# Mixture-of-experts layer behind a cross attention: first units of four experts taken from the first six batches

## The reference, cut to what matters

```python
x = x + xattn(layernorm(x), ctx, ctx, ctx)          # x: 8 x 100 x 512, ctx: 8 x 722 x 512
x = x + ffn(layernorm(x), router_w, w1, b1, w2, b2)

def xattn(x, w1, v1, w2):
    h = gelu_tanh(einsum('eth,efh->etf', x, w1)) * einsum('eth,efh->etf', x, v1)
    return einsum('etf,efh->eth', h, w2)

def ffn(h, router_w, w1, b1, w2, b2):               # 16 experts, w1: 512 x 1024, w2: 1024 x 512 each
    logits = x @ router_w                           # x: 800 tokens x 512
    assign = argmax(logits)                         # one expert for each token
    w = sigmoid(logits[assign])
    return w * (gelu(x @ w1[assign] + b1[assign]) @ w2[assign] + b2[assign])
```

## Time and profile before

| | |
|---|---|
| median of 3 runs | 310.06 us (309.59 to 310.96) |
| the profiled execution | 313.14 us, its span 311.4 us |
| TensorE | 246.1 us busy, 79% of the span |
| VectorE / GpSimd / ScalarE | 120.0 / 98.8 / 32.1 us busy |
| moved by DMA | 100.41 MB, mean 322 GB/s |
| mean granted TensorE clock | 0.917 of full speed |

### The profile page before, as it was taken

One profiled execution on the slowest core, in us unless ns is written; L12 is line 12 of the kernel. 1 busy time (PEld: TensorE's weight loads), 2 busy tenths in 40 slices (PEclk: granted clock), 3 DMA queues, 4 the chain that ended last, 5 costly groups with the idle time before them and its releaser, 6 DMA issues.

```text
span 311.4 us, 10067 instructions
## 1 busy us (share of the span) xinstructions
PE 246.1 (79%) x3668; PEld 172.9 (56%) x3669; DVE 120.0 (39%) x405; ACT 32.1 (10%) x75; POOL 98.8 (32%) x141
## 2 busy tenths in 40 slices
PE   0899999999999884397778877987984678859850
PEld 0858768768678351154456665655663456536540
DVE  3034536446444466133334333444433134324320
ACT  0411111021021120010010101010110011000100
POOL 2002314224123155003523334435343133241353
PEclk9999999999999955597999979999999599977995
DMA  7999799999999994089699968999999999999910
GB/s 258 370 372 355 271 343 360 372 309 408 336 394 380 400 376 160 26 290 385 200 352 378 372 221 302 355 367 364 378 362 388 361 422 362 390 361 388 354 36 21
DMA packets 20698, 100.41 MB, mean 322 GB/s; under 512 B 5232, under 2 KB 6224, under 8 KB 11464
## 3 DMA queue, kind: packets, MB, share of 16 engines
q1 hardware_dynamic: 15044, 93.02, 81.2%
q0 software_dynamic: 4928, 6.60, 6.7%
q10 hardware_dynamic: 708, 0.55, 0.6%
HBM read 95.58 MB, written 4.97 MB: 323 GB/s over the span
## 4 chain that ended last, share of the span: by engine, by line
PE 47%; DMA 24%; issue 10%; SPq 9%; DVE 2%; POOL 2%; POOLq 2%; ACTq 2%; DVEq 1%; ACT 0%
PE bank L308 14%; PE bank L315 14%; DMA W<-in_w 10%; DMA area<-rows 10%; PE bank L396 8%; SPq L228 8%; PE bank L385 5%; PE bank L323 2%; DMA id_out<-tok_at 2%; DMA rows<-nothing,pad_at 1%; ACTq L209 1%; PE bank L404 1%; PE bank L293 1%; PE bank L299 1%; DMA xs<-in_x 1%
## 5 line engine op out<-in xcount | busy, mean ns | idle before, releaser
L385 PE MATMUL bank<-W,area 128*32 128x256 f32 x992 | 66.5, 405 | 23.2 <-DMA W<-in_w 12.0
L396 PE MATMUL bank<-W,area 128*32 128x128 f32 x1984 | 65.8, 287 | 3.9 <-issue 3.0
L396 PEld LDWEIGHTS bank<-W,area 128*32 128x32 f32 x1984 | 56.0, 115 | 9.2 <-issue 4.2
L795 POOL DMA_INDIRECT out<-area,at_out x32 | 32.7, 1022 | 85.5 <-DVE area L672 49.4
L385 PEld LDWEIGHTS bank<-W,area 128*32 128x32 f32 x992 | 34.1, 115 | 45.4 <-issue 25.6
L315 PE MATMUL bank<-area,hidT 128*100 128x512 f32 (+1 forms) x96 | 46.8, 601 | 0.0
L308 PEld LDWEIGHTS bank<-xnT,area 128*128 128x128 f32 (+1 forms) x384 | 44.3, 193 | 4.3 <-issue 4.3
L308 PE MATMUL bank<-xnT,area 128*128 128x100 f32 (+1 forms) x384 | 44.6, 278 | 1.0 <-issue 1.0
L491 ACT ACTIVATE area<-area 128x256 f32<-128x256 f32 x31 | 12.9, 416 | 172.5 <-PE bank L396 150.7
L209 POOL DMA_DIRECT2D area<-rows x32 | 24.5, 765 | 18.3 <-issue 18.2
L672 DVE SCALAR_TENSOR_TENSOR area<-bank,area 128x128 f32 x31 | 10.9, 351 | 42.7 <-PE bank L396 24.5
(11 more groups left out here) (86 smaller groups left out, 156.4 us busy)
## 6 DMA issues: line engine op xcount, KB each, us to landing
W<-in_w SPq DMA_DIRECT2D x64, 1024.0 KB, 18.6
area<-in_ctx_main SPq DMA_DIRECT2D x8, 1280.0 KB
area<-in_ctxT_a SPq DMA_DIRECT2D x8, 768.0 KB, 10.0
area<-in_ctxT_b SPq DMA_DIRECT2D x8, 676.0 KB, 9.2
area<-rows POOLq DMA_DIRECT2D x32, 65.5 KB, 7.2
xs<-in_x SPq DMA_DIRECT2D x8, 200.0 KB
area<-in_ctx_rest SPq DMA_DIRECT2D x8, 160.0 KB
out<-area,at_out POOLq DMA_INDIRECT x32
```

The lines of the kernel that those rows point to most:

```text
L385: last = nc.tensor.matmul(p_h[U * q:U * q + U, 0:FQ], curT[:, U * k:U * k + U], mine, start=(k == 0), stop=(k == KD - 1), tile_position=(0 ...
L396: last = nc.tensor.matmul(p_y[U * q:U * q + U, 0:DQ], hT[:, U * c:U * c + U], W2[:, slot, c, DQ * q:DQ * q + DQ], start=(c == 0), stop=(c ...
L795: nc.gpsimd.indirect_dma_start(out_q, bass.IndirectOffsetOnAxis(ap=at_out[r][:, :], axis=0), y_out[:, r, :], None, bounds_check=last_out, ...
```

## The change

- **Head units.** When batches 0 to 5 are routed, the first 32 rows of experts 0 to 3 are fixed as units 0 to 3 (where an expert has fewer than 32 by then, `end_head` raises its counter so that later tokens go behind them; rows that nobody filled were zeroed at the start). GpSimd loads them in the batch loop, and their steps stand between the steps of the last batch's routing on TensorE, VectorE and ScalarE.
- **Plan.** The planned units follow as units 4 and up: experts 0 to 3 have at least one more each. The plan is computed on 44 partitions at once, and `colof` and its tables are gone.
- **Output index.** Each row carries the index of its output row, so `tok_at`, its scatters and the load of `id_out` are gone. `XW` grows from 131 to 132.
- **Row loads.** SyncE, not GpSimd, loads the rows of the planned units, expert by expert, before the weights of this expert.
- **Weights.** All 16 early halves are issued in the batch loop (`EARLY` ends in 7, not 2).
- **Tail.** Nothing is loaded behind the last unit. GpSimd handles the last one or two units through a third output buffer, one after the other.

With the counts above experts 0 to 3 now have 3, 2, 2 and 5 units (before: 3, 1, 2 and 5), the others as before, so there are 32 units.

The diff, cut to its core:

```diff
-EARLY = (0, 0, 1, 1, 1, 2, 4, 2)
+EARLY = (0, 0, 1, 1, 1, 2, 4, 7)
...
         @block.sync
...
+            def load_rows(e, slot, head):
+                at = slice(e, e + 1) if isinstance(e, int) else bass.ds(e, 1)
+                n = sp.value_load(n_i[0:1, at], min_val=1, max_val=PER)
+                start = sp.value_load(starts[0:1, at], min_val=SLOTS, max_val=MAXU - 1)
+                with sp.Fori(0, n) as u:
...
+                    sp.dma_start(xr[:, bass.ds(at, 1), :].rearrange("p o d -> p (o d)"),
+                                 rows[bass.ds(CAP * e + U * u + (U if head else 0), U), :].rearrange(
+                                     "t (q d) -> q t d", q=Q)).then_inc(s_rows[slot], 16)
+
+            def rows_landed(e, slot):
+                at = slice(e, e + 1) if isinstance(e, int) else bass.ds(e, 1)
+                sp.wait_ge(s_rows[slot], sp.value_load(slot_n[0:1, at], min_val=16, max_val=16 * MAXU))
+                sp.sem_inc(s_land, 1)
+
             sp.wait_ge(s_att, NB)
-            load_weights(2)
-            sp.wait_ge(s_land, AHEAD)
-            load_weights(4 * SLOTS - sum(EARLY) - 2)
-
-
+            sp.wait_ge(s_b2ps, len(p_b2))
             sp.wait_ge(s_plan, 1)
+            for i in range(2):
+                sp.wait_ge(s_row[i], 16 * (NB // 2))
+            for e in range(SLOTS):
+                sp.wait_ge(s_pad[e // Q], 16)
+                load_rows(e, e, True)
+                if e > 0:
+                    rows_landed(e - 1, e - 1)
+            for i in range(1, PADS):
+                sp.wait_ge(s_pad[i], 16)
+
+
             with sp.Fori(1, E // SLOTS) as g:
                 for s in range(SLOTS):
...
+                    load_rows(sp.snap(SLOTS * g + s), s, False)
                     sp.wait_ge(s_hp, before)
+                    apart()
+                    rows_landed(SLOTS * g + (s - 1), (s - 1) % SLOTS)
                     load_half(W1[:, s], first, s_w1[s], 0)
                     load_half(W1[:, s], first, s_w1[s], 1)
                     sp.wait_ge(s_y, before + 1)
+                    apart()
                     load_half(W2[:, s], second, s_w2[s], 0)
                     load_half(W2[:, s], second, s_w2[s], 1)
+            rows_landed(E - 1, SLOTS - 1)
...
         @block.tensor
...
-            transpose_x2(NB - 1)
-            logits(NB - 1)
-            ranks(NB - 1)
-            nc.tensor.matmul(p_lg[:, 0:E], ones, hot_sum[:, :], start=True, stop=False)
-            nc.tensor.matmul(p_lg[:, 0:E], ones, hot[:, :], start=False, stop=True).then_inc(s_cntps, 1)
...
+            pe.sem_inc(s_y, 1)
             transpose_tokens(0)
-            pe.wait_ge(s_tab, 7)
-            pe.sem_inc(s_y, 1)
+            pe.wait_ge(s_b2, 16)
+            spread_b2(0)
+            first_layer(0, 0, 16)
+            transpose_x2(NB - 1)
+            transpose_tokens(1)
+            spread_b2(1)
+            logits(NB - 1)
+            first_layer(1, 1, 16)
+            ranks(NB - 1)
+            nc.tensor.matmul(p_lg[:, 0:E], ones, hot_sum[:, :], start=True, stop=False)
+            nc.tensor.matmul(p_lg[:, 0:E], ones, hot[:, :], start=False, stop=True).then_inc(s_cntps, 1)
+            transpose_tokens(2)
+            spread_b2(2)
+            pe.wait_ge(s_b2v, 1)
+            spread_b2(3)
+            second_layer(0, 0, 16)
+            first_layer(2, 2, 16)
+            transpose_tokens(3)
+            second_layer(1, 1, 16)
+            first_layer(3, 3, 16)
+            pe.wait_ge(s_tab, 9)
+            pe.wait_ge(s_pos, NB)
+            nc.tensor.transpose(p_rk[0:1, 0:MAXU], done_n[:, :], ident[0:MAXU, 0:MAXU]).then_inc(s_eofps, 1)
+            second_layer(2, 2, 16)
+            transpose_tokens(4)
+            pe.wait_ge(s_plan, 1)
...
         @block.scalar
...
             copy_rows(p_t, tT, s_tps, s_tT, NB - 1)
             gate_tanh(NB - 1)
...
+            nc.scalar.activation(warm[:, :], con[0:1, 0:1], ACT.Gelu)
+            for j in range(3):
+                gelu_unit(j)
+            act.wait_ge(s_plan, 1)
+            n = units(act)
+            with act.Fori(3, n) as j:
+                gelu_unit(j)
...
         @block.vector
...
+            def end_head():
+                dve.wait_ge(s_headps, 1)
+                nc.vector.tensor_scalar(short[:, :], p_rk[0:1, 0:SLOTS], -1.0, float(U), ALU.mult, ALU.add
+                                        ).then_inc(s_short, 1)
...
+            next_tokens(0)
+            residual(NB - 1)
+            tokens(0)
+            x2_moments(NB - 1)
+            b2_copy(0)
+            next_tokens(1)
+            hidden_units(0)
+            tokens(1)
...
+            biases(0)
+            next_tokens(2)
+            b2_copy(1)
+            route(NB - 1)
+            hidden_units(1)
+            place(NB - 1)
+            pads()
+            tokens(2)
+            biases(1)
+            finish(0, 0)
+            next_tokens(3)
+            plan()
+            hidden_units(2)
+            tokens(3)
+            biases(2)
+            experts()
+            finish(1, 1)
...
+            b2_copy(2)
+            b2_copy(3)
+            next_tokens(4)
+            hidden_units(3)
+            tokens(4)
+            biases(3)
+            finish(2, 0)
...
         @block.gpsimd
...
+                if b == HEAD_END:
+
+                    pool.wait_ge(s_att, HEAD_END + 1)
+                    for i in range(2):
+                        pool.wait_ge(s_row[i], 16 * (HEAD_END // 2))
+                        apart()
+                    for e in range(SLOTS):
+                        pool.dma_start(xr[:, e, :], rows[CAP * e:CAP * e + U, :].rearrange("t (q d) -> q t d", q=Q)
+                                       ).then_inc(s_pre[e], 16)
...
-            unit(0, None, 0)
-            unit(1, None, 1)
-            pairs = pool.snap((n + 1) // 2)
+            for r in range(2):
+                scatter_unit(r, r, None)
+            pool.wait_ge(s_plan, 1)
...
+            with pool.Fori(0, left) as k:
+                scatter_unit(2 * pairs + k, 2, None)
+                pool.wait_ge(s_done[2], 16 * k + 16)
+                apart()
```

More of the change, by code:

```diff
@@ L123, in build @@
         pos = [sb(f"pos{i}", [T, 1], U32) for i in range(2)]
[L124 to L130, removed]
+        short = sb("short", [1, SLOTS])
@@ new lines, in build @@
+        need, end_f = sb("need", [MAXU, E]), sb("end_f", [MAXU, E])
+        done, done_n = sb("done", [MAXU, E]), sb("done_n", [MAXU, 1])
+        n_i, ends, starts = sb("n_i", [MAXU, E], I32), sb("ends", [1, E], I32), sb("starts", [1, E], I32)
+        slot_f, slot_n = sb("slot_f", [1, E]), sb("slot_n", [1, E], I32)
+        eof, last_but_two = sb("eof", [1, MAXU], I32), sb("last_but_two", [1, 1], I32)
+        last_unit, out_at = sb("last_unit", [1, 1], I32), [sb(f"out_at{i}", [P, 1], U32) for i in range(3)]
@@ L151, in build, with part @@
[L151 to L154, removed]
+        used = 0
+        def part(n):
+            nonlocal used
+            used += n
+            return area[:, used - n:used]
+        cur, curT = part(DQ), part(KD * U)
+        h_pre, hT = part(KF * U), part(KF * U)
+        y_out = part(3 * DQ).rearrange("p (r d) -> p r d", r=3)
@@ L579, in _ @@
                     place(b - 1)
-                residual(b)
+                if b + 1 < NB:
+                    residual(b)
+                    x2_moments(b)
                 if b == 0:
@@ L701, in _ @@
             biases(last + 1)
-            finish(last)
-            next_tokens(last + 3)
+            finish(last, dve.snap(last % 2))
+            dve.sem_inc(s_next, 1)
             hidden_units(last + 2)
             biases(last + 2)
-            finish(last + 1)
-            finish(last + 2)
-            n = units(dve)
-            dve.wait_ge(s_sent, n)
-            dve.sem_inc(s_yo, 1)
+            finish(last + 1, dve.snap(last % 2 + 1))
+            finish(last + 2, 2)
         @block.gpsimd
@@ L806, in _ @@
+            with pool.Fori(1, pairs) as i:
+                for r in range(2):
+                    scatter_unit(2 * i + r, r, 16 * i)
+            with pool.Fori(0, left) as k:
+                scatter_unit(2 * pairs + k, 2, None)
+                pool.wait_ge(s_done[2], 16 * k + 16)
+                apart()
             for r in range(2):
-                pool.wait_ge(s_ld[r], 16 * pairs)
-                apart()
                 pool.wait_ge(s_done[r], 16 * pairs)
```

350 lines of the change are left out of this document (150 added, 200 removed).

## The result

The changed kernel takes 326.15 us (median of four runs, 324.49 to 329.4) against 310.51 for the kernel before in the same rounds: a ratio of 1.048, interval 1.042 to 1.055. It is slower, by more than twice what was forecast. Its profiled execution took 325.96 us with a span of 324.0; the forecast for that span was 318.3. Executions of a kernel over 1.5% above its fastest are left out of every ratio in this document, so that a median beside a ratio can seem too high for it: of the three edits together two of four executions remain, of the five edits four of twelve, of the six edits three of ten.

A forecast was written before the change was run, and what follows sets the result against it. The prediction took the DMA stream of weights and context, with holes, as the bound. Restart 149.5 + hole 1.1 + 48 x 2.93 + row loads 16.2 = 307.4, plus tail 10.9 = 318.3; by ratio 317, range 302.5 to 321.5.

The forecast's parts named there:

- restart: SyncE's first weight issue after the early halves, behind head units and plan: at 149.5 us, bounds 144 and 154.
- holes after it, and row loads on four engines: Weight stream after its restart: a 1.1 us hole, plus 16.2 us for row loads carried by only four engines.
- 48 halves: Weight halves streamed after the restart, 2.93 us each without row loads: 140.6 us.
- tail: From the stream's end to the span's end, last outputs and scatters: 10.9 us against 15.9, between 8 and 14.
- TensorE, not the stream, ends last: End of the kernel: a sign named in advance that would show the prediction wrong; no size given.
- Two units of expert 0, then one of expert 1, then `rows_landed(0)`: SyncE's row loads before the restart: three, 2 us each, signal at 139, first layer of unit 4 from 141.3.
- Slot 3 is free after six more units, 26 us; 12 halves last 35. So 7.3 of 8.4 us of holes go: Weight stream after the restart: slot 3 comes free before twelve halves have passed, removing 7.3 of 8.4 us of holes.
- Rival 4: SyncE's queue: rows queue behind weights and TensorE waits; some 330 us; chance 0.12 together with Rival 3.
- Rival 1: Weight stream: row loads spread over the engines; end 305.3, by ratio 304 us; chance 0.25.
- 2: Stream restart: hardly moves (144) and row loads spread; 300 us, median 298.5; chance 0.08.
- 5: Whole kernel: nearly cancels, four engines at 0.69 and restart at 146; 311.8 us; chance 0.10.
- Rival 3: Head: half clock throughout, restart late at 154, and four engines; 323 us, median 321.5; chance 0.12 together with Rival 4.

The follow-up runs named there:

- the three edits together: Changed kernel with expert read moved ahead of the output wait, last batch's routing first, and ScalarE loading expert 3's rows: 312.58 to 320.93 us, no ratio.
- the five edits: Changed kernel with read moved, routing first, expert 3's rows by ScalarE, SyncE's signal earlier, own output buffer for the last unit: 312.78 us, ratio 0.995.
- the six edits: Changed kernel with the five edits plus each SyncE row load issued as four transfers of 32 partitions: ratio 0.999, median of all ten 316.87 us.
- the run with pieces: Changed kernel with each SyncE row load issued as four transfers of 32 partitions, nothing else: 325.28 us, ratio 1.042.
- the moved read: Changed kernel with VectorE's register read of the next tokens' expert put in front of the wait for the output: 321.21 us, ratio 1.033.
- the four edits together: Changed kernel with the three edits together plus SyncE's rows wait and signal to VectorE moved ahead of the next expert's row loads: 314.67 us, ratio 1.012.
- the fifth: Adds to the four edits together an output buffer of its own for the last unit: 312.78 us over 12 runs, ratio 0.995.

## Why the prediction was wrong

With the 2.83 of that run the changed kernel's span can be added up, the stream taken to the last packet of the weights at 307.0: 156.1 + 48 x 2.83 (135.8) leaves 15.1 for holes and the slow four engines together. Term by term, against the forecast's 318.3:

| term | forecast | measured | difference |
|---|---|---|---|
| restart | 149.5 | 156.1 | +6.6 |
| holes after it, and row loads on four engines | 1.1 + 16.2 | 15.1 | -2.2 |
| 48 halves | 140.6 | 135.8 | -4.8 |
| tail | 10.9 | 17.0 | +6.1 |
| span | 318.3 | 324.0 | +5.7 |

The 15.1 can be divided only in part: 4.7 of it are the four engines' time behind the fall of the share at 302.3, and the rest is in the fourteen 10 us stretches from 156 to 296, of which those below a share of 1.00 lack 10.4 us together. The sign was right, and the stream's end too (307.4 and 307.0). But the latter was luck: the restart is 6.6 off, the halves 4.8 the other way, and the stream doesn't set the end at all, since TensorE no longer waits for a weight half. That is the forecast's own sign of being wrong: "TensorE, not the stream, ends last".

*"Two units of expert 0, then one of expert 1, then `rows_landed(0)`": restart.* The head's times held within about 1 us up to the plan (132.9, forecast 132). The step failed behind it: `load_rows` runs for experts 0 to 3 before the first weights, nine loads instead of the three that I counted (though "19 of the 28 loads come after the restart" counts the nine). The signal for expert 0 still came after the third, at 141.1 (139), so TensorE was soon through: unit 5's first layer ended at 151.2, and SyncE was late by 4.9. The step mattered less than I thought, though. A restart 2.3 earlier gave nothing, and one 12.3 later, in the run with pieces, cost nothing that its cheaper row loads didn't give back.

*"Slot 3 is free after six more units, 26 us; 12 halves last 35. So 7.3 of 8.4 us of holes go": the step that failed.* The six units took 41.2 us, from 151.2 to 192.5, and the sum closes: six at 4.57 are 27.4 (a little more than the 26), the two stands of 5.36 and 4.06 are 9.4, and the half clock behind them costs 4.4. The forecast had a warning in its own rows: in the kernel before the eight units between 140.36 and 186.40 took 46.0, 5.8 each and not 4.3. From 156.1 to the request it was 37.6 us; twelve halves last 34 at 2.83, so the queues ran dry (0.55 at 186 to 196), as they had in the kernel before.

The 4.57 come from a register read in `next_tokens` that I didn't count. Alone on the kernel before it cost nearly nothing, where other waits cover it; in the changed kernel moving it gave 4.4 us at the request and 5.6 at the end. The stands are on TensorE's first passes through the loop, 6.9 more than in the kernel before. That these are fetches of instructions behind a full queue is argued from the packets' times, and the packets that have no gap beside them speak against it; no run tried it, and it stays open. The place of the routing is the other part that a run shows: with it first the request came 6.8 earlier and the end 6.4.

A simple reading of the whole follows. The profiled executions differ by 12.6 us (324.0 and 311.4; the medians by 15.6). The request is 7.3 later, and there TensorE sets the time; the other 5.3 lie behind it. From request to end it is 125.0 us before and 130.3 after; 129.1, 130.7, 132.6, 128.6, 128.9 and 127.3 in the six runs from the moved read to the four edits together; 124.4 with the five, 128.5 with pieces and 121.5 with the six. So this part isn't a constant. Behind the request TensorE waits for tokens, VectorE for SyncE's signal, and SyncE stands in a full queue: the stream sets the pace there through SyncE, not through weights that arrive late. An early half or an early restart ahead of the request is worth nothing unless TensorE comes earlier too. That fits why the change's own gain was not seen: it loads sooner what TensorE can't yet release.

*Four engines, 16.2 us.* The mechanism is shown (13.5 us for 24 loads, 0.56 each, in a full stream) and it is at work in the changed kernel: a share of 0.28 at 190 to 192, of 0.30 at 303 to 306, and four late landing signals for each of the last halves. Its place in the sum was wrong. By 0.56 the 19 loads would cost 10.6 us of a full stream; but the queues ran dry in between, and the waits view has no wait of TensorE for a half's late part. In pieces the loads brought nothing in the times, neither on the changed kernel nor on the five edits.

*Halves, 2.93.* They took 2.83. Why that is 0.1 less than the kernel before let one work out was not tried.

*Tail, 10.9.* It was 17.0 from the last packet of the weights (the terms as listed give 11.2). W1 of expert 14 is complete at 291.0, 16 before the stream's end, as forecast. The second layer of unit 30 ends at 311.0, 20 behind it and not 18: units follow at 4.57, not 3.9, and TensorE begins those from 284.25 on only after the 6.5 us wait for the signal. The two outputs and scatters take 7.0 and not 6.1; the buffer that they share was in the forecast. After the last scatter there are 6.0 us, not 3.1. So 2.0, 0.9 and 2.9 make the difference; the 2.9 stay open. From the last packet of the weights to the span's end the four edits leave 13.9 and the fifth 11.5.

*The rivals.* Rival 4 came true in part: rows queue on SyncE behind weights, VectorE waited 26.9 us for their signal, and TensorE 16.7 us with it. Changing the signal's order gave 1.4 us, by no means the sum. But no run took all row loads off SyncE's queue, as in the kernel before, with the rest of the change in place; what this wait costs is therefore not shown. Rival 1 is out, since the loads don't spread (13.5 us between the two shapes), and 2 and 5 are, since the restart was late. Rival 3's size was about right and its reason not: what made the restart late was SyncE's row loads. The half clock came where no rival had it, behind the two stands of TensorE.

## What to carry to other kernels

In a stream with few slots, find the request that waits longest for the consumer, and time the consumer's path to it from the old trace, waits included, not from the shortest unit in it. Work moved ahead of that request is worth only what it moves the request itself. Price a slower unit at each place where units stand on that path, not once. And do not add the full price of a slow transfer to that of a hole: a transfer that fills only some engines costs most where the queues are full (0.56 us each here), and little that these runs can tell from nothing where they run dry anyway.

## What the runs showed of the hardware

- A transfer of 64 KB with a slowest dimension of 4 costs a full stream of weights 0.56 us more than the same bytes with 128 there (24 of them: 13.5 us, share 0.89 against 1.03). In the changed kernel, whose row loads have this shape, the last four of a half's sixteen landing signals come up to 4.4 us behind the twelfth; in the kernel before, 0.8 at most (the halves of experts 12 to 15).
- Nine row loads in loops on SyncE took 19.42 us, 2.2 on average with the reading of registers; within one expert the next starts 1.3 us behind (two in 1.96, the last issue 0.66 of it). With the queue full, three took 6.79 us, and what stands behind them on SyncE, signals too, waits as long.
- A register read from memory ahead of a wait on VectorE adds 0.67 us to the gap (0.95 against 0.28); read ahead of the output instead, where VectorE waits anyway, it leaves a gap of 0.24.
- On its first passes through the loop TensorE stood 5.36 and 4.06 us, with one packet of 0.02 MB on the instruction queue beside each; such packets also stand where it has no such gap. The granted clock was 0.50 in the 3 us behind the first (164 to 167), and a first layer took 3.51 us instead of 1.93.
